# Full-height contraction of the decay matmuls and half-size weight folds in an mLSTM and mixture-of-experts block

## What is computed

```
xn = layernorm(x)                                 # (16, 256, 128)
q, k, v = block-diagonal maps of xn; ig, fg = 3 * xn @ w + b per head
cs = cumsum(log_sigmoid(fg))
log_D[s,t] = cs[s] - cs[t] + ig[t]   for t <= s, else -inf
D = exp(log_D - max_t log_D)
C = (q k^T / sqrt(32)) * D
s = headnorm(C / (max(|sum C|, exp(-max)) + eps) @ v) * (1 + ln_w)
e = argmax(softmax(xn @ router_w + router_b))      # one expert per token
y = (a * sigmoid(g)) @ w2[e] + b2[e],  [a, g] = xn @ w1[e] + b1[e]
out = x + s * silu(y)
```

## Time and profile before

| | |
|---|---|
| times of three runs | 250.81, 251.05, 248.66 us (median 250.81) |
| the profiled execution | 249.57 us |
| its span, first to last instruction | 247.5 us |
| PE busy | 211.2 us, 85% of the span |
| PE weight loads | 172.4 us, 70% |
| DVE busy | 178.7 us, 72% |
| ACT busy | 124.4 us, 50% |
| POOL busy | 103.3 us, 42% |
| mean granted TensorE clock | 0.963 of 2.4 GHz |

### The profile page before, as it was taken

The page is one execution under the profiler, slowest core; times in us unless marked ns, Lnnn a source line. Parts: engine busy times, 40 slices in busy tenths (PEclk is TensorE's granted clock), DMA queues, the critical chain, the costliest instruction groups (busy, mean ns, idle before and its releaser), DMA issues.

```text
span 247.5 us, 5928 instructions
## 1 busy us (share of the span) xinstructions
PE 211.2 (85%) x1811; PEld 172.4 (70%) x1819; DVE 178.7 (72%) x474; ACT 124.4 (50%) x287; POOL 103.3 (42%) x127
## 2 busy tenths in 40 slices
PE   0788878598999889977999998999999999999730
PEld 0677743244565555647999998999999999996400
DVE  3987297645658869865877978797889888672390
ACT  1179577135555455547555654655565556640120
POOL 7526602344445446520043346334643454466060
PEclk9979999659999999999999999999999999999996
DMA  6799992282013799532001293201120210000794
GB/s 172 215 201 153 250 415 81 58 213 102 28 45 107 219 247 255 198 98 56 0 33 56 56 317 83 61 22 52 49 62 20 53 54 33 17 21 11 217 316 146
DMA packets 37756, 29.67 MB, mean 120 GB/s; under 512 B 3419, under 2 KB 34403, under 8 KB 37725
## 3 DMA queue, kind: packets, MB, share of 16 engines
q1 hardware_dynamic: 34286, 24.98, 39.3%
q0 software_dynamic: 2272, 4.22, 4.9%
q10 hardware_dynamic: 1168, 0.10, 0.3%
HBM read 20.20 MB, written 9.54 MB: 120 GB/s over the span
## 4 chain that ended last, share of the span: by engine, by line
PE 69%; issue 7%; DMA 6%; DVE 5%; ACT 5%; POOL 1%; ACTq 1%; SPq 1%; DVEq 1%; POOLq 0%
PE bank L1128 12%; PE bank L1137 12%; PE head_bank L1128 12%; PE bank L1075 7%; PE bank L1055 5%; PE head_bank L1065 5%; PE bank L1086 4%; PE head_bank L976 3%; PE bank L1054 3%; DMA nat<-in_L_attn_wk 2%; DMA xw<-y_tokens 2%; PE bank L961 2%; PE head_bank L1041 2%; PE bank L952 1%; DVE ra L641 1%
## 5 line engine op out<-in xcount | busy, mean ns | idle before, releaser
L450 POOL DMA_INDIRECT y_tokens<-ffn,xs_sb x39 | 38.9, 997 | 72.8 <-DVE ffn L924 71.9
L445 POOL DMA_INDIRECT xs_sorted<-xw,pos x32 | 31.6, 988 | 35.2 <-PE head_bank L1065 23.3
L1137 PE MATMUL bank<-w_sb,dm 128*128 x312 | 41.4, 276 | 1.2 <-DVE dm L908 1.2
L1137 PEld LDWEIGHTS bank<-w_sb,dm 128*128 128x128 f32 x312 | 38.0, 192 | 1.6 <-issue 1.6
L1128 PE MATMUL bank<-xsT,wc 128*128 128x128 f32 x320 | 39.1, 275 | 0.0
L1128 PEld LDWEIGHTS bank<-xsT,wc 128*128 128x128 f32 x320 | 37.3, 192 | 0.0
L1128 PE MATMUL head_bank<-xsT,wc 128*128 128x128 f32 x304 | 37.0, 275 | 0.0
L805 DVE TENSOR_TENSOR cm<-dm,head_bank 128x1024 f32<-128x1024 f32 (+1 forms) x32 | 29.1, 949 | 10.3 <-PE head_bank L1065 8.9
L1128 PEld LDWEIGHTS head_bank<-xsT,wc 128*128 128x128 f32 x304 | 35.4, 192 | 0.0
L563 ACT ACTIVATE dm<-bank 128x512 f32<-128x512 f32 x48 | 26.9, 596 | 15.8 <-PE bank L1055 12.9
L586 ACT ACTIVATE wc<-w_sb 128x512 f32 x39 | 24.6, 630 | 15.1 <-issue 15.1
(11 more groups left out here) (187 smaller groups left out, 347.4 us busy)
## 6 DMA issues: line engine op xcount, KB each, us to landing
w_sb<-in_L_ffn_w SPq DMA_DIRECT2D x12, 512.0 KB, 12.4
x_sb<-in_L_attn_x SPq DMA_DIRECT2D x16, 256.0 KB, 4.9
wc<-in_L_ffn_w SPq DMA_DIRECT2D x8, 512.0 KB
xs_sorted<-pad_row SPq DMA_DIRECT2D x1, 2515.5 KB, 23.5
xs_sb<-xs_sorted SPq DMA_DIRECT2D x13, 193.5 KB, 2.7
xw<-y_tokens SPq DMA_DIRECT2D x8, 256.0 KB, 4.5
out_x<-xw SPq DMA_DIRECT2D x8, 256.0 KB, 3.2
y_tokens<-ffn,xs_sb POOLq DMA_INDIRECT x39
```

Of the source, the lines that this page charges most:

```text
L445: pool.indirect_dma_start(xs_dram, bass.IndirectOffsetOnAxis(ap=pos[:, t:t + 1], axis=0), xw[:, t, :], None).then_inc(s_scat, 16)
L450: pool.indirect_dma_start(y_dram, bass.IndirectOffsetOnAxis(ap=xs_sb[:, j // CH % NX, j % CH, D:DW].bitcast(I32), axis=0), ys_sb[:, j // C ...
L1137: last = pe.matmul(bank[6 + j % 2][:, 0:D], uT[:, j % 2, c, :], w2_sb[:, bass.ds(e * (HC * D) + c * D, D)], start=(c == 0), stop=(c == HC ...
```

## The change

`left` gets one slot per batch instead of one per batch of a strip: it grows from [128, 4, 256] to [128, 16, 256], still bfloat16. It is set to 0 instead of 1 (by POOL, in one memset), and four DVE memsets set the ones: strip i (32 partitions) in the slots of its four batches, 1024 elements in each partition. They stand behind `evac_vl(9)` and ahead of the gate arithmetic. SP waits for them (`s_lone`) before it loads `left`. The indicator `ind` in `right` now is 1 only in the first 12 partitions of each strip. With that, the decay matmuls of batches 4 to 15 contract all 128 partitions: outside the batch's own strip `left` is 0. Batches 0 to 3 keep their 15 rows. PE waits for the DMAs of the strips 1 to 3 together, ahead of batch 4.

`fold_row(e)` becomes `fold_half(k)`, k from 0 to 15: half an expert's 1024 columns, 512 of them, one half behind the outputs of each turn from b = 1 on, and the last behind turn 15. Every second half counts `s_sub`.

```diff
-        left = sb("left", [P, NBS, S], BF16)
+        left = sb("left", [P, B, S], BF16)
...
             sp.wait_ge(s_left, 2)
+            sp.wait_ge(s_lone, 4)
...
-                sp.dma_start(left[32 * i:32 * i + 3 * NH, :, :],
+                sp.dma_start(left[32 * i:32 * i + 3 * NH, NBS * i:NBS * (i + 1), :],
...
-            pool.memset(left[:, :, :], 1.0).then_inc(s_left, 1)
+            pool.memset(left[:, :, :], 0.0).then_inc(s_left, 1)
...
-            dve.tensor_reduce(ind[:, :], ident[:, :].rearrange("p (g h) -> p h g", h=NH), AX.X, ALU.add).then_inc(s_ind, 1)
+            dve.tensor_reduce(ind[:, :], ident[:, :].rearrange("p (i g h) -> p h i g", i=4, h=NH)[:, :, :, 0:3], AX.XY, ALU.add).then_inc(s_ind, 1)
...
             evac_vl(9)
+            dve.wait_ge(s_left, 1)
+            for i in range(4):
+                dve.memset(left[32 * i:32 * (i + 1), NBS * i:NBS * (i + 1), :], 1.0).then_inc(s_lone, 1)
...
-                    if 6 <= b < 6 + E:
-                        fold_row(b - 6)
+                    if b >= 1:
+                        fold_half(b - 1)
+                fold_half(B - 1)
                 outputs(B - 1)
...
-            def fold_row(e):
-                if e == 0:
+            def fold_half(k):
+                e, cols = k // 2, slice(k % 2 * HID, (k % 2 + 1) * HID)
+                if k == 0:
                     dve.wait_ge(s_w1, 16 * E)
                 dve.wait_ge(s_bc[e % 3], 16 * (e // 3 + 1))
-                w = w1_sb[0:P - 1, e, :]
-                dve.tensor_tensor(w, w, last_row[0:P - 1, e % 3, :], ALU.subtract).then_inc(s_sub, 1)
+                w = w1_sb[0:P - 1, e, cols]
+                done = dve.tensor_tensor(w, w, last_row[0:P - 1, e % 3, cols], ALU.subtract)
+                if k % 2 == 1:
+                    done.then_inc(s_sub, 1)
...
-                rows = slice(32 * i, 32 * i + 3 * NH + 3)
+                rows = slice(0, 3 * NH + 3) if i == 0 else slice(0, P)
...
-                pe.matmul(bank[n % 2][:, :], left[rows, j, s0:s0 + P], right[rows, :, j, t0:t0 + P],
+                pe.matmul(bank[n % 2][:, :], left[rows, b, s0:s0 + P], right[rows, :, j, t0:t0 + P],
```

More of the change, by code:

```diff
@@ L242, in mlstm_moe_block @@
         s_dummy = sem("s_dummy")
+        s_lone = sem("s_lone")
         s_y0 = sem("s_y0")
@@ L1050, in log_decay @@
                     pe.wait_ge(s_dm, n - 1)
-                if j == 0 and m == 0:
-                    pe.wait_ge(s_lr[i], 32)
+                if n == 0:
+                    pe.wait_ge(s_lr[0], 32)
+                if i == 1 and j == 0 and m == 0:
+                    for strip in range(1, 4):
+                        pe.wait_ge(s_lr[strip], 32)
                 if m != 1:
                     pe.matmul(bank[n % 2][:, :], ident_bf[:, :], maskn[:, :, :].rearrange("p h t -> p (h t)"), start=True, stop=False)
-                pe.matmul(bank[n % 2][:, :], left[rows, j, s0:s0 + P], right[rows, :, j, t0:t0 + P],
+                pe.matmul(bank[n % 2][:, :], left[rows, b, s0:s0 + P], right[rows, :, j, t0:t0 + P],
                           start=(m == 1), stop=True).then_inc(s_ld, 1)
```

## The result

| | before | after |
|---|---|---|
| median | 250.34 us (4 executions) | 258.85 us (257.52 to 262.42, 4 executions) |
| ratio | | 1.033, 95% interval 1.025 to 1.041 |
| the profiled execution | 249.57 us, span 247.5 | 262.42 us, span 260.3 |
| mean granted clock | 0.963 | 0.931 |

The forecast was 254.2 us, with a range to 256.8. The sign was right and the size was not: the change costs 8.3 us (3.3% of 250.3), twice the 4.2 of the sum. The ratio is taken over fast executions alone and leaves out the 262.42 us one, which counts as slow; so 8.3 is a little less than the 8.5 us between the medians. The profiled execution of the changed kernel is the longest of its four and 3.6 us above their median, so a stage read from it shows the place of the loss, and its size rather too large.

A forecast was written before the change was run, and what follows sets the result against it. PE was taken to bound attention's turns, and a slackless chain over DVE, ACT, POOL and DMA the stage ahead. 4.0 + 2.0 - 1.2 - 1.5 + 0.9 = +4.2 us on 250.0 gave 254.2 us, range 250.8 to 256.8.

The forecast's parts named there:

- wide decays: Decay matmuls over 128 rows in attention: mask to decay drops 0.32 to 0.22 us, 0.10 net per turn, -1.2 us.
- half folds: Attention's eight fold turns: a half fits DVE's 0.89 us gap where a whole fold delays weigh and scores, -1.5 us.
- the clock in attention: Low clock at attention's start, already there before: may end sooner or later by chance, about 1 us either way.
- The memsets: Four DVE memsets at the gate chain's head: 1.07 us each, less 0.3 us of slack, +4.0 us.
- The clock at the gate sums: PE's idle ahead of the gate sums grows from 1.61 to 5.6 us, the clock falls, +2.0 us.
- The forecast's two bounds: 128-row decays: -2.3 us if the step to token_rows also shortens, +1.4 if scores loses its whole overlap.
- The end of attention: Two half folds behind the outputs of turn 14 delay `s_sub`, so PE starts the experts +0.9 us later.
- Rival C: Clock falls again where attention ends, ahead of the experts: about 2 us more, 256.2 us; chance 0.09.
- Rival A: DVE memsets as fast as a 429 ns copy, clock may stay up: -0.4 us, 249.6 us; chance 0.14.
- B: Clock stays up at the gate sums and attention gains all it can: +1.1 us, 251.1 us; chance 0.11.
- D: 128-row decays make scores lose its overlap, +1.4 instead of -1.2 us: 256.8 us; chance 0.04.

The follow-up runs named there:

- warm_gate: Changed kernel plus 13 dummy matmuls of 256 columns in PE's idle ahead of the gate sums: 254.23 us, against 257.9 for the changed kernel in its group.
- all_warm: Changed kernel plus dummy matmuls in both PE idle stretches, 13 ahead of the gate sums and 6 ahead of attention: 254.42 us, ratio 1.014 to the kernel before.
- before_warm2: Kernel before plus six dummy matmuls ahead of the first decay matmul, second run of that kernel: 250.15 us, ratio 0.996 to the kernel before.
- halves_only: Kernel before with folds in halves and nothing else: 248.91 us, ratio 1.012 to the kernel before.
- halves_warm: halves_only plus five dummy matmuls between attention and the experts: 251.06 us, ratio 1.002 to the kernel before.
- memsets_only: Kernel before plus the four DVE memsets of ones ahead of the gate arithmetic: 254.76 us against 246.08 before.
- fixed_wide: Kernel before with 128-row decays, whole folds; POOL sets zeros and ones as float32 behind its copy, no DVE memset: 247.21 us, ratio 1.001 to before.
- wide_only: Kernel before with decays of batches 4 to 15 over 128 rows, ones written by POOL, whole folds: 255.28 us, ratio 1.033 to before.
- ones_on_pool: Changed kernel with the four memsets of ones on POOL instead of DVE: 256.19 us, ratio 1.038.
- after_again: Changed kernel once more, unedited, beside variants on another chip: 257.9 us against 246.43 for the kernel before.
- before_warm3: Kernel before plus six dummy matmuls ahead of attention, third run of that kernel: 249.15 us, ratio 0.987 to the kernel before.
- wide_warm: fixed_wide plus six dummy matmuls ahead of attention: 248.52 us, ratio 0.989 to the kernel before.
- wide_warm3: The wide_warm kernel again, in a group with more rounds: 248.63 us, ratio 0.989 to the kernel before.
- repaired_warm: 128-row decays and half folds, with fixed_wide's POOL order and dummy matmuls ahead of attention and of the experts: 250.87 us, ratio 0.995 to before.

## Why the prediction was off, point by point

Two steps failed. The larger is the pair of gains: -1.2 for the wide decays and -1.5 for the half folds came to 0 or worse, which is 2.7 of the 4.1 us between forecast and measurement. The other is the clock in attention, which the sum had at nothing.

**The memsets: right.** +4.0 forecast, 4.28 measured; the mechanism (queued behind them on DVE, no slack in the chain) held. The rate was nearly right: 1.18 us from one memset to the next, for 1.07 forecast. The Trainium skill ("VectorE: DVE Perf Modes", section "Zero memsets can be issued as uint32 (trn2)"), with one cycle per element, gave an estimate of 4.3 us for the four; at 1.18 us each they took 4.7, so the trace agrees to about a tenth.

**The clock at the gate sums: right in place and size.** +2.0 forecast, 1.68 measured on the sums, 1.47 by the start of attention; warm_gate shows it is the idle that does it.

**The clock in attention: a step that failed.** The forecast said of the low level there "by chance it can end sooner or later in any execution, which is about 1 us either way in the range". In the profiled execution it ended 12 us later behind the first decay matmul than before and cost 4.4 us, one way and not either way. How much of the 8.3 us it is, is less sure, since that execution is the longest. An estimate from the mean clocks and the two levels: the fastest execution (span 255.4 us, clock 0.95) ran 25.5 us at the low level, the kernel before 18.3 (247.5 us, 0.963). The difference of 7.2 us is hardly more than the 6.8 at the gate sums in the profile, so that execution may have lost nothing more in attention, and it still was 7.2 us above the median of before. The other two come to 30 and 31 us at the low level. With the clock held up in both kernels (all_warm, before_warm2) the change loses 4.3 us, 3 us either way; of the 4.0 less than 8.3, about 1.5 belong to the gate sums.

When the low level ends, by all profiles without dummies ahead of attention:

| profile | decays | low clock at the gate sums, us | low clock ends after the first decay matmul, us |
|---|---|---|---|
| before | narrow | 0 | 8.9 |
| halves_only | narrow | 0 | 9.6 |
| halves_warm | narrow | 0 | 9.4 |
| memsets_only | narrow | 3.4 | 10.5 |
| warm_gate | wide | 0 | 14.7 |
| fixed_wide | wide | 0 | 15.0 |
| wide_only | wide | 6.8 | 14.5 |
| ones_on_pool | wide | 6.8 | 14.7 |
| after | wide | 6.8 | 20.9 |
| after_again | wide | 6.8 | 21.0 |

A low clock at the gate sums is not needed for a long stretch, as warm_gate and fixed_wide show. All six wide profiles are longer than all four narrow ones, but the first 128-row decay comes with batch 4, when the stretch is over in all six (in after it ends at 74.47 us and the first 128-row decay starts at 75.42). So the height of the matmuls is not the reason, and what is stays open. The long executions of memsets_only, with narrow decays, were timed and not profiled.

**Decays over 128 rows, -1.2: a step that failed, it is 0 or a loss.** Mask to decay was right (0.22), and the loss at scores was put at 0.10 where the step itself grew by 0.30. The forecast's two bounds were both true at once: token_rows came 0.10 earlier and scores lost its whole overlap, and with the later mask they cancel. On the chips of the first result and of the last two groups the turn also closes over ACT, and there plain wide turns are 0.1 us longer. From values_sum(2) to (14) the profiles on those chips have 45.5 (before), 44.7 (before_warm2) and 45.4 (before_warm3) with narrow decays and whole folds, 46.1 (wide_warm) and 45.5 (wide_warm3) with wide ones. The Trainium skill ("TensorE: Matmul & The Clock Gate", Part 3, section "The mechanism") says that a weight load overlaps running matmuls only where the row group differs. By that mask to decay would have stayed 0.32; the rows show 0.22, so the measurement decides against it here.

**Half folds, -1.5: a step that failed, it is 0 or a loss.** (The +0.8 at the end of attention is the forecast's own +0.9.) The 1.5 us lost before in the eight fold turns do not come from a fold that is too long: with half folds the twelve turns take 44.6 us in halves_warm, with whole ones 44.7 in before_warm2, on one chip. (With wide decays the half folds have the longer turns: 46.9 in all_warm against 46.1 in wide_warm, 46.6 in repaired_warm against 45.5 in wide_warm3, one profile each.) Four of the five long fold turns are turns in which ACT starts `evac_u` late. ACT in the kernel before, two turns of the fold stretch:

```profile
90.91 0.38 ACT L570 ACTIVATE uTs<-bank 128x256 f32<-128x256 f32 x1 [1.64 <-PE bank L1075]
...
94.13 0.39 ACT L570 ACTIVATE uTs<-bank 128x256 f32<-128x256 f32 x1 [0.90 <-PE bank L1075]
```

The first starts 1.69 us behind the start of its values_sum, the second 0.95, and DVE runs a whole fold in both; one turn took 3.96 us and the next 3.55. The longest turn, 4.36 us from 84.86, starts `evac_u` in time; there ACT's exponential comes late, after 1.07 us of idle:

```profile
87.28 1.08 ACT L563 ACTIVATE dm<-bank 128x512 f32<-128x512 f32 x2 [1.07 <-PE bank L1055]
```

Two late starts of `evac_u` in before stand ahead of the first fold, one of them at low clock. The changed kernel has the same late starts with half folds (1.66 us idle), in 5 of its 12 turns at full clock, and no profile of the first two groups has any at full clock, whole folds or not. The forecast read a coincidence in time, folds and long turns, as a cause. What makes ACT late was not found.

**The end of attention: right,** 0.77 for 0.9. Rival C was given 0.09 and did come, in halves_only and four others with half folds; it cost 0.9 to 1.7 us in halves_only. It did not come in the profiled execution of the changed kernel, and it came in five profiles with whole folds too.

**The sum.** The gains that did not come are 2.7 of the 4.1 us missing. The losses that were forecast, 6.9, came to 6.5 (4.28, 1.47, 0.77). What is left, 1.8, is the clock in attention and turns that grew longer; no run parts the two on the chip of the first result. The sign was right because the memsets and the gate sums outweighed everything else. Rival A (fast memsets) and B (clock stays up) fell with the first rows. D named a true mechanism, the lost overlap, but not what paid it back.

## What to carry to other kernels

A small delay ahead of an engine that then idles is not paid once: here 4.3 us of memsets brought 1.5 us more at the gate sums, because the clock fell in the idle. So look at every idle stretch of PE ahead of a dense stage: six dummy matmuls there made the kernel before 0.4 to 1.3% faster in three runs, the smallest of them within the noise, the only gain in this study. And a saving inside one engine's turn counts only after following the loop through the others: that is where 2.7 us of forecast gain went; a busy share of 97% does not say that the engine sets the turn.

## What the runs showed of the hardware

- DVE instructions with both inputs in SBUF stood still for as long as POOL's CAST ran: L719 4.15 us instead of 0.67, done 0.6 us after the CAST. In fixed_wide the last of POOL's memsets ran until 31.00 us beside the same additions, which started at 30.77 and took their 0.67. The Trainium skill ("SBUF — State Buffer", section "Who interferes with whom") says this: such a DVE instruction contends with a GpSimd instruction that reads SBUF, not with one that only writes it. The trace agrees.
- Behind a 512-column decay matmul over 128 rows the 32-row matmuls of scores start 0.31 us after it; behind one over 15 rows, 0.01 us. And mask to decay is 0.1 us shorter from 128 to 128 rows than from 128 to 15.
- On POOL a memset costs by elements: 128x4096 bfloat16 3.51 us, the same bytes as 2048 float32 1.80 us. On DVE 32x1024 bfloat16 took 1.18 us from start to start; no float32 memset was run there.
